# Expert loops of a macaron block on Trainium2: one count per tile from TensorE instead of four

## The reference

```python
def ffn(x, router_w, router_b, w1, w2):            # x: 2048 x 128, after a layer norm
    route = softmax(x @ router_w + router_b, axis=1)
    max_prob, max_ind = max(route, axis=1), argmax(route, axis=1)
    for e in range(8):                             # w1[e]: 128 x 1024, w2[e]: 512 x 128
        a, g = split(x @ w1[e], 2, axis=1)
        y = silu(a) * g @ w2[e]
        out = where(max_ind == e, y, out)
    return out * max_prob
x = x + 0.5 * ffn(layernorm(x), ...)
x = x + state_space(layernorm(x), ...)
x = x + 0.5 * ffn(layernorm(x), ...)
```

## Time and profile before

| | us |
|---|---|
| median of 3 runs | 420.73 |
| lowest, highest | 418.76, 422.01 |
| the profiled execution | 421.93 |
| its span in the profile | 420.2 |
| first expert loop, first turn to last scatter's end | 28.57 to 102.1 |
| second expert loop | 344.10 to 418.3 |

### The profile page before, as it was taken

How to read it: one execution, slowest core, us unless ns; L and a number is a source line. 1 busy time by engine, 2 the same in 40 slices (tenths; PEclk the granted TensorE clock), 3 DMA queues, 4 the chain that set the end, 5 groups by cost and what they waited for, 6 DMA issues and landing times.

```text
span 420.2 us, 8465 instructions
## 1 busy us (share of the span) xinstructions
PE 376.4 (90%) x2962; PEld 341.6 (81%) x2962; DVE 310.0 (74%) x475; ACT 262.2 (62%) x508; POOL 260.1 (62%) x190
## 2 busy tenths in 40 slices
PE   8398999995898988999999899999998388999996
PEld 7298999995764477899998789999898387998996
DVE  4744455462799699999999999999969754555462
ACT  3315333340497999999999999999645414343331
POOL 7044677653001009999999999999960044666654
PEclk9679999999699999999999999999999679999999
DMA  7926621210930269544444345444236222121210
GB/s 210 341 55 184 168 60 45 48 33 32 369 132 4 47 153 18 176 137 126 135 159 147 125 145 156 139 128 141 98 135 268 62 64 38 38 47 40 47 39 32
DMA packets 42730, 47.47 MB, mean 113 GB/s; under 512 B 13313, under 2 KB 34370, under 8 KB 42178
## 3 DMA queue, kind: packets, MB, share of 16 engines
q1 hardware_dynamic: 37634, 39.72, 32.1%
q0 software_dynamic: 2944, 6.13, 6.1%
q10 hardware_dynamic: 2112, 1.08, 1.1%
HBM read 37.38 MB, written 9.54 MB: 112 GB/s over the span
## 4 chain that ended last, share of the span: by engine, by line
ACT 28%; PE 26%; DVE 11%; POOL 5%; issue 4%; DMA 1%; DVEq 0%; POOLq 0%; ACTq 0%
ACT phase L1051 12%; ACT phase L1061 10%; PE psum L661 9%; DVE phase L967 8%; PE psum L673 5%; POOL w_sb L884 4%; PE psum L336 2%; PE psum L1184 2%; PE psum L1454 2%; PE psum L1464 2%; PE psum L604 1%; ACT dt L921 1%; PE psum L1152 1%; POOL phase L374 1%; DMA phase<-token_rows,token_row 1%
## 5 line engine op out<-in xcount | busy, mean ns | idle before, releaser
L884 POOL TENSOR_TENSOR w_sb<-phase,w_sb 128x1024 f32<-128x1024 f32 x62 | 144.6, 2454 | 0.0
L967 DVE TENSOR_TENSOR_SCAN phase<-phase,psum 128x1024 f32<-128x1024 f32 x64 | 142.4, 2272 | 2.7 <-PE psum L1134 2.3
L661 PE MATMUL psum<-phase 128*128 128x128 f32 x736 | 92.9, 277 | 4.3 <-issue 2.4
L661 PEld LDWEIGHTS psum<-phase 128*128 128x128 f32 x736 | 87.1, 192 | 6.4 <-issue 4.0
L374 POOL DMA_INDIRECT phase<-token_rows,token_row x46 | 46.6, 1013 | 56.9 <-DVE token_row L476 27.4
L1051 ACT ACTIVATE phase<-dtxT,B_cols 128x256 f32<-128x256 f32 x192 | 79.9, 499 | 0.2
L1152 PE MATMUL psum<-ident,w_sb 128*128 128x128 f32 x512 | 67.5, 276 | 3.3 <-DVE silu_z L960 0.9
L1061 ACT ACTIVATE phase<-dt,neg_A 128x1024 f32<-128x1024 f32 x64 | 69.8, 1139 | 0.0
L497 DVE TENSOR_TENSOR phase<-phase,psum 128x512 f32<-128x512 f32 x46 | 31.5, 684 | 46.4 <-PE psum L661 21.8
L1152 PEld LDWEIGHTS psum<-ident,w_sb 128*128 128x128 f32 x512 | 56.5, 141 | 8.6 <-POOL w_sb L884 6.9
L566 ACT ACTIVATE phase<-psum 128x512 f32<-128x512 f32 x46 | 27.3, 594 | 54.7 <-PE psum L661 34.6
(11 more groups left out here) (180 smaller groups left out, 402.5 us busy)
## 6 DMA issues: line engine op xcount, KB each, us to landing
w_sb<-c_rows SPq DMA_DIRECT2D x32, 512.0 KB, 3.9
w_sb<-ffn_w SPq DMA_DIRECT2D x16, 512.0 KB, 7.3
B_diag<-dt SPq DMA_DIRECT2D x4, 1024.0 KB, 10.1
phase<-B_diag SPq DMA_DIRECT2D x32, 128.0 KB, 3.9
w_sb<-ffn_w SPq DMA_DIRECT2D x8, 256.0 KB, 7.4
token_rows<-x_tok SPq DMA_DIRECT2D x4, 264.0 KB, 5.0
token_rows<-x_tok ACTq DMA_DIRECT2D x4, 264.0 KB, 6.1
x_tok<-attn_x SPq DMA_DIRECT2D x4, 256.0 KB, 4.6
```

The source lines that it names most:

```text
L661: last = nc.tensor.matmul(psum[:, 2 * k + part, c * P:(c + 1) * P], w1_tile[:, t % W1_RING, part * F + c * P:part * F + (c + 1) * P], xsT_ ...
L884: nc.gpsimd.tensor_tensor(hC[:, k % HC_RING, :], H[:, k % H_RING, :], C_sb[:, j % C_RING, :], ALU.mult).then_inc(M["hC_ready"], 1)
L967: nc.vector.tensor_tensor_scan(H[:, k % H_RING, :], dA[:, k % DECAY_RING, :], dBx_bank[k % SLOTS], 0.0, ALU.mult, ALU.add).then_inc(M["sca ...
```

## The change

TensorE's four semaphores per tile become one, `tile_done`, which it raises once at the end of each turn of its loop. The turn moves behind the down projection, so that it is mostly the last matmul and carries the count. The first three turns have a semaphore of their own, `xsT_first`; the last tile still counts each piece, five counts in all. The other engines' waits are translated by `hidden_a`, `hidden_g`, `down_done` and `wait_turned` into values of `tile_done`. VectorE's order in the loop becomes give(t-2), gate(t), pick(t+3) instead of pick(t+2), gate(t), give(t-2), with three picks ahead of the loop. On ScalarE norm(3) moves into the loop, behind silu(0) and turn(2).

```diff
-                "xsT_psum", "xsT_ready", "w1_ready", "h_a", "h_g", "gate_ready", "u_ready", "ys_psum",
-                "ys_ready")}
+                "xsT_first", "xsT_ready", "w1_ready", "tile_done", "gate_ready", "u_ready", "ys_ready")}
...
+        END = SLOT_TILES - 1
+
+        def hidden_a(t):
+            return t + 1
+
+        def hidden_g(t):
+            return t + 1 if t < END else END + 3
+
+        def down_done(t):
+            return t + LAG + 1 if t < END - LAG else (END + 2, END + 4, END + 5)[t - END + LAG]
+
+        def wait_turned(engine, f, t):
+            if t <= LAG:
+                engine.wait_ge(f["xsT_first"], t + 1)
+            else:
+                engine.wait_ge(f["tile_done"], t - LAG + 1)
...
                 dve.wait_ge(f["gate_ready"], t + 1)
-                dve.wait_ge(f["h_g"], t + 1)
+                dve.wait_ge(f["tile_done"], hidden_g(t))
                 if t >= U_RING:
-                    dve.wait_ge(f["ys_psum"], t - U_RING + 1)
+                    dve.wait_ge(f["tile_done"], down_done(t - U_RING))
...
             def give(t):
 
-                dve.wait_ge(f["ys_psum"], t + 1)
+                dve.wait_ge(f["tile_done"], down_done(t))
...
-            for t in range(W1_RING - 1):
+            for t in range(W1_RING):
                 pick(t)
-            for t in range(SLOT_TILES - 1):
-                if t + W1_RING - 1 < SLOT_TILES:
-                    pick(t + W1_RING - 1)
-                gate(t)
+            for t in range(END):
                 if t >= LAG:
                     give(t - LAG)
-            give(SLOT_TILES - 3)
-            gate(SLOT_TILES - 1)
-            give(SLOT_TILES - 2)
-            give(SLOT_TILES - 1)
+                gate(t)
+                if t + W1_RING < SLOT_TILES:
+                    pick(t + W1_RING)
+            give(END - 2)
+            gate(END)
+            give(END - 1)
+            give(END)
...
             def turn(t):
 
-                act.wait_ge(f["xsT_psum"], t + 1)
+                wait_turned(act, f, t)
                 if t >= TURN_RING:
-                    act.wait_ge(f["h_g"], t - TURN_RING + 1)
+                    act.wait_ge(f["tile_done"], hidden_g(t - TURN_RING))
...
             def silu(t):
-                act.wait_ge(f["h_a"], t + 1)
+                act.wait_ge(f["tile_done"], hidden_a(t))
...
             norm(2)
-            norm(3)
             for t in range(SLOT_TILES):
                 silu(t)
                 if t + 2 < SLOT_TILES:
                     turn(t + 2)
+                if t == 0:
+                    norm(3)
...
-            turn(0)
-            for t in range(SLOT_TILES - 1):
+                return last
+
+            turn(0).then_inc(f["xsT_first"], 1)
+            for t in range(END):
                 hidden(t, 0)
-                if not t:
-                    turn(1)
-                hidden(t, 1)
-                if t + 2 < SLOT_TILES:
-                    turn(t + 2)
+                if t < LAG:
+                    turn(t + 1).then_inc(f["xsT_first"], 1)
+                last = hidden(t, 1)
                 if t >= LAG:
-                    down(t - LAG)
-            hidden(SLOT_TILES - 1, 0)
-            down(SLOT_TILES - 3)
-            hidden(SLOT_TILES - 1, 1)
-            down(SLOT_TILES - 2)
-            down(SLOT_TILES - 1)
+                    last = down(t - LAG)
+                if LAG < t + LAG < SLOT_TILES:
+                    last = turn(t + LAG)
+                last.then_inc(f["tile_done"], 1)
+            hidden(END, 0).then_inc(f["tile_done"], 1)
+            down(END - 2).then_inc(f["tile_done"], 1)
+            hidden(END, 1).then_inc(f["tile_done"], 1)
+            down(END - 1).then_inc(f["tile_done"], 1)
+            down(END).then_inc(f["tile_done"], 1)
```

More of the change, by code:

```diff
@@ L486, in pick @@
                 if t >= W1_RING:
-                    dve.wait_ge(f["h_g"], t - W1_RING + 1)
+                    dve.wait_ge(f["tile_done"], hidden_g(t - W1_RING))
                 nc.vector.tensor_copy(w1_tile[:, t % W1_RING, :], w1_sb[:, ds(e * (2 * F), 2 * F)]).then_inc(f["w1_ready"], 1)
@@ L549, in norm @@
                 if t >= NORM_RING:
-                    act.wait_ge(f["xsT_psum"], t - NORM_RING + 1)
+                    wait_turned(act, f, t - NORM_RING)
                 xs = xs_sb[:, t % XS_RING, :]
@@ L648, in turn @@
                     pe.wait_ge(f["xsT_ready"], t - 1)
-                nc.tensor.transpose(xsT_bank(t), xsn_sb[:, t % NORM_RING, :], ident[:]).then_inc(f["xsT_psum"], 1)
+                return nc.tensor.transpose(xsT_bank(t), xsn_sb[:, t % NORM_RING, :], ident[:])
             def hidden(t, part):
@@ L663, in hidden @@
                                             xsT_sb[:, t % TURN_RING, :], start=True, stop=True)
-                last.then_inc(f["h_g" if part else "h_a"], 1)
+                return last
             def down(t):
@@ L674, in down @@
                                             w2_sb[:, ds(e * (FC * D) + c * D, D)], start=(c == 0), stop=(c == FC - 1))
-                last.then_inc(f["ys_psum"], 1)
-            turn(0)
-            for t in range(SLOT_TILES - 1):
+                return last
+            turn(0).then_inc(f["xsT_first"], 1)
+            for t in range(END):
                 hidden(t, 0)
-                if not t:
-                    turn(1)
-                hidden(t, 1)
-                if t + 2 < SLOT_TILES:
-                    turn(t + 2)
-                if t >= LAG:
-                    down(t - LAG)
-            hidden(SLOT_TILES - 1, 0)
-            down(SLOT_TILES - 3)
-            hidden(SLOT_TILES - 1, 1)
-            down(SLOT_TILES - 2)
-            down(SLOT_TILES - 1)
+                if t < LAG:
+                    turn(t + 1).then_inc(f["xsT_first"], 1)
+                last = hidden(t, 1)
+                if t >= LAG:
+                    last = down(t - LAG)
[7 more added lines that the diff above has]
+            down(END).then_inc(f["tile_done"], 1)
         with nc.Block(no_gpsimd_drain=True) as block:
```

## The result

| | before, us | after, us |
|---|---|---|
| median | 420.97 | 424.36 |
| lowest, highest (20 runs each) | 418.74, 422.61 | 420.68, 427.89 |
| profiled execution, its span | 421.93, 420.2 | 422.39, 420.6 |

After stands to before as 1.0065, with an interval of 1.0043 to 1.0087: slower by 0.65%, where 411 us and "faster" had been forecast. Two slow runs of after, 427.19 and 427.89 us, are left out of this ratio but not of the table. The median lies 0.4 us beyond the upper end of the range, 424.

A forecast was written before the change was run, and what follows sets the result against it. TensorE was taken to bound the kernel, with 12.17 us of holes from late counts. 421.9 less 9.1 (holes) and 1.0 (starts) gave 411.8, 410.6 in medians, forecast 411; range 407 to 415, to 424 for 8 in 10.

The forecast's parts named there:

- Counts: Expert loops: one count per 2.79 us instead of four, below the 1.5 to 2.2 us service rate, so no growing queue.
- Residual: Loss left in both loops by late counts: 0.3 us on a third of 34 tiles, about 3.1 of 12.17 us.
- the first in line stays late: Rival: each lone count stays late, costing 0.3 to 0.46 us on all 34 tiles; 417 to 424 us, chance 0.18.
- the blocking rival: Rival: gathers block counts until TensorE idles ahead of a tile's first half, 1.4 us per two tiles; 432 us, chance 0.11.
- TensorE's own issue: Rival: holes come from register loads between down-projection records, so only the starts gain; about 421 us, chance 0.07 with another rival.
- Slack: Single count through silu and turn copy to TensorE's next first half: 0.99 us of a 2.79 us tile, leaving 1.80 us.
- Order of down and turn: TensorE's loop: turn moved behind the down projection, same records, expert-number load still covered by 1.79 us of matmuls; nothing.
- VectorE's new order: VectorE's give, multiply and pick end about 2.3 us after the count, under 2.79, hidden; third pick in prologue costs nothing.
- tail: Last tile keeps separate counts; only the previous tile's silu starts 0.9 us later, wanted 2.7 us later; nothing.
- The 26 ns per count: Skill's rule that matmul increments serialize: 124 fewer worth 3.3 us, 418.6 us; 0.07 chance together with another cause.
- Start: Start of each loop: norm(3) behind silu(0) and turn(2), third tile starts earlier; 1.0 us gain together, -0.5 to 2.0.
- GpSimd as the bound: Rival: gather plus scatter take 2.77 us per tile; stretched by 0.1 us they lose 3 us; 413.6 us, chance 0.07.

The follow-up runs named there:

- up_after: Changed kernel with all 23 gathers issued ahead of the first scatter, rings of 23 and 16: 451.99 us, 1.0713 of before.
- half_before: Kernel before, token rows read in order, odd tiles' gathers made plain loads on GpSimd's queue, even ones still indirect: 407.23 us, 0.9668 of before.
- hw_after: Changed kernel, token rows read in order, gathers made plain loads from ScalarE's queue, 7 tiles ahead: 407.49 us, 0.9620 of before.
- half_after: Changed kernel, token rows read in order, odd tiles' gathers made plain loads on GpSimd's queue: 407.57 us, 0.9671 of before.
- after_again: Changed kernel unaltered, measured again on another chip: 407.08 us, 0.9970 of before, which took 408.5 to 408.9 us in these last comparisons.
- orders_only: Kernel before with the new orders of VectorE, ScalarE and TensorE but still four counts per tile: 423.16 us, 1.0045 of before.
- selfp_before: Kernel before, its gathers also waiting for a silu so that GpSimd pauses when a count is late, another chip: 408.85 us, 1.0003 of before.
- counts_only: Kernel before with its old orders but one count per tile, behind the down projection: 424.52 us, 1.0087 of before.

## Why the prediction was wrong

**The step that failed** is *Counts*, and with it the *Residual*: "One per 2.79 us is below that rate, four are above it. So I expect no growing queue", from which 3.1 us of holes were to remain of 12.17. (Its own sum, 0.3 us on a third of 34 tiles, is 3.4, which changes nothing.) In the two middles, where 8.76 us of holes stood, 8.28 remained, and the starts lost 1.0 us more. The counts are not served at a rate. With one count per tile the count is 2.5 us late (56.83 to 59.33), as late as the first in line was before (2.26 us), and 20 us late in up_after with the same number of counts. "So lateness wants three things here: dense matmuls, frequent counts, and gathers running" was right about the third alone. Density and frequency were read from one stretch, where all three came together; the stretch behind the last gather had the same density and the same four counts and was prompt, so it had already spoken against frequency.

**The step ahead of it** does not hold either: "Why the holes? The other engines are not late by their own work; TensorE's counts reach them late." The counts were late, but in the middles they were hardly what made the holes: about 7.8 of 8.76 us lay between records of w1 and of the down projection, where TensorE waits for no count. Of the two holes at the starts only that of loop one was a wait, 1.31 us; loop two's lay inside the down projection, from 351.40 to 354.08. So fewer counts had little there to save even if each had been prompt. Late counts and gaps in TensorE's stream come and go together: both are there while indirect gathers run, both are gone in half_before and behind the last gather. The change moved part of the loss from the one to the other. How a gather does either is not shown by any run here.

**The rival "the first in line stays late"** comes nearest: 417 to 424 us at a chance of 0.18, measured 424.36. Its step holds where it applies: lateness 2.5 less slack 1.80 is 0.7 us per hole, and the holes ahead of the tiles at 53.78, 60.13, 66.47 and 72.83 are 0.76 to 0.87 us by the turns (56.56, 62.91 and their like come 3.55 to 3.66 us behind the turn ahead instead of 2.79). Its sum does not hold: it had 10.2 to 15.6 us from all 34 tiles, and the waits ahead of w1 come to 4.4 us in both middles. The rest of the 8.28 us is gaps in TensorE's stream, and the starts lost where it had a gain of 1.0. That the total came near is in part luck. Nor had it the rhythm: in this stretch only every second tile pays. That was the mark of the blocking rival, "that hole serves two tiles"; but there a count was to come only when TensorE stood still, and the one of 59.33 came 0.3 us before that, so a pair of tiles pays 0.8 us and not 1.4, and 432 us was too much. The rival "TensorE's own issue", near 421 us at 0.07 together with the rule, had the place of before's holes right and the reason wrong: w1 has gaps too, without a register load between its records, and they go with the gathers.

**Slack** (1.80 us) was right, 1.8 us in hw_after. **Order of down and turn, VectorE's new order, tail: nothing** was right: hw_after and half_after are within 0.7 us of their partners, as far as four runs each can tell. **The 26 ns per count** that the Trainium skill ("TensorE: Matmul & The Clock Gate", section "The cost: per-tile semaphore tail") gives for increments by matmuls, which would have made 124 fewer counts worth some 3.3 us, is not to be seen in TensorE's stream: with prompt counts a record takes 0.111 us both with four counts per tile (481 in 53.40 us, half_before) and with one (506 in 56.20, after_again). In the two pairs with prompt counts the kernel with fewer counts was 0.7 and 0.3 us slower.

**Start** (1.0 us of gain, -0.5 to 2.0) had its sign wrong where counts are late. Turn 3 does start 0.57 us earlier, at 33.38 instead of 33.95, but TensorE then meets GpSimd's run of gathers earlier and stands 0.93 us longer behind it. From the first record of w1 to the fifth tile's first, loop one takes 12.61 us instead of 12.02 and loop two 12.61 instead of 12.16, a loss of 1.0 us in the profiled executions where a gain of 1.0 was forecast. I had named that end ("silu(1) held behind it") and put it at 0.5 us; it did not count that a longer stop can cost the clock. In orders_only the longer hole of loop two comes with 6.8 us at half clock. Where the counts are prompt the term is about right in sum: after_again takes 1.4 us less than before, and 1.3 us of that can be read in loop one's start. A trace of before was not taken there; in selfp_before, which took the same time as before, TensorE waits ahead of the third turn, which in the old order stands before the second tile's first half:

```profile
32.43 0.33 PE L652 MATMUL psum<-ident,phase 128*128 128x128 f32 x1 [1.16 <-ACT phase L555]
```

and after_again starts that turn at 31.85 without a wait. From the first record of w1 to the fifth tile's first it is 10.97 us there and 9.66 in after_again; in loop two both take 9.66.

**GpSimd as the bound** fell: in the middle of after_again TensorE is full with every gather and scatter in place.

**The median against the profiled execution.** By their spans the two differ by 0.4 us: the starts take 0.59 and 0.45 us more and the first middle 0.30, the second middle 0.78 less. The other 3 us of the medians come from the spread of after's runs. That a fall of the clock follows a hole is shown by the traces of orders_only and counts_only; that such falls make the spread of after's runs is argued from their mean clocks, and no trace shows it.

## What to carry to other kernels

A wait that ends "remote", long after the work it waits for, was here no cost of counting: look for what other queue is running at that time, and for a stretch of the same trace where it isn't. And a late count costs nothing until somebody stands still for it: before pricing it, find each hole of the busy engine and see whether a wait stands there. Test with the suspected traffic in another form before spending work on the number of semaphores; here, where counts were late, the form of the gathers was worth 13 to 16 us and the number of counts no gain. Bundling counts takes slack from every reader, so it is to be tried only where counts are prompt, and a tuning step of 0.5% should be measured on more than one chip: this one is +0.65% on some and -0.30% on others.

## What the runs showed of the hardware

In all comparisons but the last two, indirect gathers issued by GpSimd came with late semaphore counts of TensorE and with gaps in its stream. The lateness ran from 1.0 us (counts_only, 67.53 to 68.52) to 5.1 us (orders_only, 347.71 to 352.80), and in a run of 23 gathers it was 20 us, with 12 records of TensorE in 12.3 us near its end. Plain loads of the same rows on the same queue did not do this, and mixing them one to one with indirect ones was enough to fill TensorE's stream. In the last two, on two other chips, the trace of the changed kernel, unaltered, showed none of it, and the kernel before took 408.5 to 408.9 us instead of 420.5 to 422.7. A hole of 4.9 us between matmuls came with 6.8 us at the lower clock level and one of 1.79 us with 3.4 us, while the hole of 2.68 us ahead of 352.24 in the profiled execution of after was not followed by any; so the length of the hole alone does not decide it.
